# The border between feed-forward and attention: where the layer-norm statistics are made, and who clears and fills the key buffers

## The reference

```
x = x + depool(...)                    # stage 1
x = x + g * ffn(layernorm(x))          # stage 2: per-batch merged weights
x = x + g * attention(layernorm(x), context keys and values)   # stage 3
x = x + g * columns(layernorm(x))      # stage 4

layernorm(x) = (x - mean) / sqrt(var + 1e-5)          # over the 256 columns
attention: qkv = x @ w_qkv.T, 16 heads of 16; k, v = [context, own] (375 + 112 rows)
           softmax(q k^T / 4) v, then @ w_proj.T + b_proj
```

## Time and profile before

| what | value |
|---|---|
| median of three executions | 1504.93 us (1501.84 to 1507.17) |
| profiled execution | 1506.88 us |
| its span | 1505.1 us |
| mean granted TensorE clock | 0.954 |
| busy TensorE, VectorE, ScalarE, GpSimd | 1360.8, 1015.7, 620.0, 546.7 us |
| stage 3 starts | 571.39 us |

### The profile page before, as it was taken

The page is one execution under the profiler, slowest core; times in us unless marked ns, Lnnn a source line. Parts: engine busy times, 40 slices in busy tenths (PEclk is TensorE's granted clock), DMA queues, the critical chain, the costliest instruction groups (busy, mean ns, idle before and its releaser), DMA issues. The chain is left out here.

```text
span 1505.1 us, 33126 instructions
## 1 busy us (share of the span) xinstructions
PE 1360.8 (90%) x12672; PEld 963.5 (64%) x12672; DVE 1015.7 (67%) x1961; ACT 620.0 (41%) x1371; POOL 546.7 (36%) x829
## 2 busy tenths in 40 slices
PE   3687999999999984899999999999999687999997
PEld 3464677777777762567776777667776463555555
DVE  6777665677556764778888888778888543444544
ACT  4433212211221112656666666656666442222221
POOL 0576888888840004323222232222231570000000
PEclk9998999999999996899999999999999688999999
DMA  8205445454531008667667777666672000000000
GB/s 243 66 1 171 132 134 165 124 165 133 162 110 41 32 1 117 123 83 95 84 85 92 97 96 91 84 83 84 84 93 24 0 1 0 13 12 12 20 17 25
DMA packets 92774, 120.25 MB, mean 80 GB/s; under 512 B 7414, under 2 KB 78899, under 8 KB 90348
## 3 DMA queue, kind: packets, MB, share of 16 engines
q1 hardware_dynamic: 83436, 87.82, 34.5%
q0 software_dynamic: 9216, 30.73, 7.0%
HBM read 96.42 MB, written 22.10 MB: 79 GB/s over the span
## 5 line engine op out<-in xcount | busy, mean ns | idle before, releaser
L1123 DVE TENSOR_REDUCE s_neg_max<-banks 112x1 bf16<-112x487 f32 x512 | 323.7, 662 | 92.5 <-PE banks L1234 89.3
L1059 ACT ACTIVATE s_prob<-banks 128x448 f32<-128x448 f32 x512 | 265.9, 547 | 180.2 <-PE banks L1256 180.0
L640 DVE TENSOR_TENSOR s_m<-banks,s_base 128x512 f32<-128x512 f32 x256 | 164.6, 685 | 129.3 <-PE banks L794 129.1
L1234 PE MATMUL banks<-s_k_t,s_q_t 96*112 96x487 bf16 x512 | 198.5, 388 | 1.5 <-DVE s_neg_max L1123 1.5
L1256 PEld LDWEIGHTS banks<-s_q_t,s_k_t 112*128 112x128 bf16 x2048 | 143.4, 99 | 82.1 <-issue 33.9
L1256 PE MATMUL banks<-s_q_t,s_k_t 112*128 112x112 bf16 x2048 | 187.2, 214 | 3.7 <-issue 3.0
L794 PE MATMUL banks<-s_gate_sel,s_tw 64*128 64x256 f32 x1024 | 147.4, 408 | 0.9 <-DVE s_m L640 0.8
L1270 PE MATMUL banks<-s_prob,s_v 128*32 128x112 f32 (+1 forms) x4096 | 129.2, 265 | 7.7 <-issue 7.7
L834 PE MATMUL banks<-s_m,s_act_t 128*112 128x256 f32 x512 | 129.8, 389 | 5.9 <-DVE x_res L659 5.8
L817 PEld LDWEIGHTS banks<-s_x_t,s_m 128*128 128x128 f32 x1024 | 119.1, 192 | 21.2 <-issue 20.9
L817 PE MATMUL banks<-s_x_t,s_m 128*128 128x112 f32 x1024 | 130.5, 281 | 0.0
(11 more groups left out here) (257 smaller groups left out, 2182.7 us busy)
## 6 DMA issues: line engine op xcount, KB each, us to landing
k_parts<-s_k_split POOLq DMA_DIRECT2D x64, 281.2 KB, 3.4
s_k_t<-k_parts SPq DMA_DIRECT2D x32, 562.5 KB, 7.7
s_tw<-in_tw SPq DMA_DIRECT2D x16, 1024.0 KB, 5.1
s_k_raw<-in_ctx_k POOLq DMA_DIRECT2D x64, 187.5 KB, 3.6
s_k_t<-k_parts SPq DMA_DIRECT2D x32, 375.0 KB, 9.9
s_v_raw<-in_ctx SPq DMA_DIRECT2D x32, 256.0 KB
s_src<-in_ctx SPq DMA_DIRECT2D x8, 896.0 KB, 14.4
s_k_t<-k_parts SPq DMA_DIRECT2D x32, 187.5 KB, 11.2
```

What stands on the lines that cost most here:

```text
L640: nc.vector.tensor_tensor(dst[:, :, :, rows_], got, base[:, :, rows_].unsqueeze(2).broadcast_to([P, 2, B, HR]), ALU.add).then_inc(S["merge ...
L1059: nc.scalar.activation(prob[t % 2][:, c, :], w.bank(SCORE + n % SRING, P, TILE), ACT.Exp, scale=DH ** -0.5).then_inc(S["exp_done"], 1)
L1123: nc.vector.tensor_reduce(neg_max[half][:, ROWS + h, 0:1], w.bank(MAX + n % MRING, T, NKEY), AX.X, ALU.max, negate=True).then_inc(S["max_d ...
L1234: nc.tensor.matmul(w.bank(MAX + n % MRING, T, NKEY), q_t[k][0:ROWS, h, :], k_t[k][0:ROWS, h, FIRST:FIRST + NKEY], start=True, stop=True).t ...
```

## The change

1. Stage 2 keeps the statistics of the first eight batches alone: after every second pair, one batch (`early_statistics`).
2. The other 24 are made in stage 3's first turns by VectorE (`late_statistics`): batches 8 to 15 behind `norm(0)`, 16 to 23 behind `split(0)`, 24 to 31 behind `evacuate_queries(0, 0)`.
3. Variance, root and inverse are made in two parts: batches 0 to 7 at the start; for the others the variance stands behind the last statistics, the root on ScalarE behind `evacuate_keys(0, 1)`, the inverse on VectorE behind `evacuate_queries(1, 1)`.
4. ScalarE does one Sqrt of one element behind stage 2's last Gelu.
5. GpSimd clears only the three key edges first, then waits for the first norm and clears the rest. VectorE's `ident16`, `b_proj` and `neg_max` stand behind the first norm.
6. The key rows of buffers 1 and 2 are filled by GpSimd behind `query_parts` of batches 0 and 1. Buffer 0 stays on ScalarE.

```diff
@@ stage 2, VectorE and ScalarE
                     for p in range(PAIRS):
                         added(c, p)
-                        if p:
-                            pair_statistics(p - 1)
-                    pair_statistics(PAIRS - 1)
+                        if p % 2:
+                            early_statistics(p // 2)
+
+                def early_statistics(b):
+                    dve.wait_ge(S["x_done"], nth(PAIRS * (FC - 1) + b // 2))
+                    chain.link(nc.vector.bn_stats(stats[:, b, :], w.x_res[:, b, :]))
+                    nc.vector.bn_aggr(w.mean_var[:, b, :], stats[:, b, :])
...
+                nc.scalar.activation(w.table[:], w.ident[:, 0:1], ACT.Sqrt)
@@ stage 3, GpSimd
                     nc.gpsimd.memset(k_t[k][0:ROWS_MAX, :, 0:FIRST], 0.0).then_inc(S["pads_cleared"], 1)
+                wait(pool, "xn_done", 1)
                 nc.gpsimd.memset(qk[:, 0:H, 6:SLOTS, :], 0.0)
...
+                    if b < 2:
+                        place_heads(b + 1)
+
+                def place_heads(k):
+                    wait(pool, "q_parts_done", k)
+                    nc.gpsimd.tensor_copy(k_t[k][ROWS:ROWS_MAX, :, FIRST:FIRST + S2],
+                                          w.ident[ROWS:ROWS_MAX, ROWS:ROWS_MAX].unsqueeze(2).broadcast_to([H, H, S2]))\
+                        .then_inc(rows_ready[k], 1)
+                    pool.wait_ge(rows_ready[k], 2)
@@ stage 3, ScalarE
+                def roots(first, end, part):
+                    wait(act, "var_done", part)
+                    nc.scalar.activation(root[:, first:end], var[:, first:end], ACT.Sqrt).then_inc(S["root_done"], 1)
+
+                roots(0, EARLY, 1)
...
-                    if b < 2:
-                        place_heads(2 * b)
+                    if b == 0:
+                        place_heads()
...
+                    if (b, n) == (0, 1):
+                        roots(EARLY, B, 2)
@@ stage 3, VectorE
+                def late_statistics(first, end):
+                    for b in range(first, end):
+                        last = nc.vector.bn_stats(late_stats[:, b - EARLY, :], w.x_res[:, b, :])
+                    chain.link(last)
+                    for b in range(first, end):
+                        last = nc.vector.bn_aggr(w.mean_var[:, b, :], late_stats[:, b - EARLY, :])
+                    chain.link(last)
+
+                variances(0, EARLY)
+                inverses(0, EARLY, 1)
...
                     normalised(nc, w, xn[b % 2][:], b).then_inc(S["xn_done"], 1)
-
-                def place_heads():
-
-                    wait(dve, "pads_cleared", 2)
-                    nc.vector.tensor_copy(k_t[1][ROWS:ROWS_MAX, :, FIRST:FIRST + S2],
-                                          w.ident[ROWS:ROWS_MAX, ROWS:ROWS_MAX].unsqueeze(2).broadcast_to([H, H, S2]))\
-                        .then_inc(rows_ready[1], 1)
+                    if b == 0:
+                        prepare()
+                        late_statistics(EARLY, 2 * EARLY)
...
                     if b == 0:
-                        place_heads()
+                        late_statistics(2 * EARLY, 3 * EARLY)
...
+                    if (b, n) == (0, 0):
+                        late_statistics(3 * EARLY, B)
+                        variances(EARLY, B)
+                    if (b, n) == (1, 1):
+                        inverses(EARLY, B, 2)
```

More of the change, by code:

```diff
@@ L56 @@
 CREDIT = 4
+EARLY = 8
 def nth(n):
@@ L134, in __init__ @@
         self.gates = sb("gates", [P, 4])
+        self.table = sb("table", [P, 1])
         self.banks = ctx.enter_context(nc.psum_tensor("banks", [P, 8, 512], F32))
@@ L894, in stage3 @@
         stats = sb("s3_stats", [T, 6])
+        late_stats = sb("s3_late_stats", [T, B - EARLY, 6])
         tmp, root, var = sb("s3_tmp", [T, B]), sb("s3_root", [T, B]), sb("s3_var", [T, B])
@@ L1001, in _, with place_heads @@
             def _(act):
[L1002 to L1008, removed]
+                def roots(first, end, part):
+                    wait(act, "var_done", part)
+                    nc.scalar.activation(root[:, first:end], var[:, first:end], ACT.Sqrt).then_inc(S["root_done"], 1)
+                roots(0, EARLY, 1)
+                def place_heads():
+                    wait(act, "pads_cleared", 1)
+                    nc.scalar.activation(k_t[0][ROWS:ROWS_MAX, :, FIRST:FIRST + S2],
                                          w.ident[ROWS:ROWS_MAX, ROWS:ROWS_MAX].unsqueeze(2).broadcast_to([H, H, S2]),
-                                         ACT.Copy).then_inc(rows_ready[k], 1)
+                                         ACT.Copy).then_inc(rows_ready[0], 1)
                 def evacuate_x(b):
@@ L1089, in _, with variances, inverses, prepare @@
                 chain = Chain(dve, S["chain"])
[L1090 to L1097, removed]
+                def variances(first, end):
+                    nc.vector.tensor_scalar(var[:, first:end], w.mean_var[:, first:end, 1], EPS, None, ALU.add)\
+                        .then_inc(S["var_done"], 1)
+                def inverses(first, end, part):
+                    at_ = slice(first, end)
+                    wait(dve, "root_done", part)
+                    wait(dve, "var_done", part)
+                    chain.link(inverse_root(nc, chain, w.rstd[:, at_, 0], root[:, at_], var[:, at_], tmp[:, at_]))
+                def late_statistics(first, end):
[7 more added lines that the diff above has]
+                inverses(0, EARLY, 1)
+                def prepare():
+                    nc.vector.tensor_copy(ident16[:], w.ident[0:T, 0:T])
+                    dve.wait_ge(w.attention_in, N_WEIGHTS)
+                    nc.vector.tensor_scalar(b_proj[:], b_proj[:], w.gates[0:T, 1:2], None, ALU.mult).then_inc(S["bias_ready"], 1)
+                    for k in range(2):
+                        last = nc.vector.memset(neg_max[k][:], 0.0)
+                    chain.link(last)
                 def norm(b):
```

## The result

The changed kernel took 1496.62 us in the median of 20 executions (1488.19 to 1510.34), the kernel before 1507.51 in 20 (1499.11 to 1520.92). The ratio is 0.992, 95% interval 0.9902 to 0.9937: some 12 us faster, where 6.9 were forecast. The kernel before thus lay 2.6 us above the median that was known ahead. The profiled execution (1503.94, span 1502.2) is one of the slowest of the 20, so I read in it where time goes at the border, not the total.

A forecast was written before the change was run, and what follows sets the result against it. TensorE, busy 90% of the span, was taken as the bound, so only its starved time at the feed-forward/attention border could be won: 8.8 + 2.3 - 1.3 - 2.9 = 6.9 us, from median 1504.93 to 1498.0; range 1492.3 to 1502.5.

The forecast's parts named there:

- Tail: End of the feed-forward: with most statistics gone, TensorE's pairs take 1.03 us instead of 1.575; gain 8.8 us.
- Head: Start of the attention up to the first normalised tile: no table load, norm undisturbed by GpSimd; gain 2.3 us.
- X: Moment the first normalised tile of the attention is ready: S + 5.13 before, forecast S + 2.8.
- S: Start of the attention, 571.39 us in the kernel before; times at its head are counted from it.
- the bound for it: Attention's start: if ScalarE loads its table again, the root starts at S + 1.28 and the gain is 1.7, not 2.3.
- X to Y: Batch 0, from X to TensorE's turning of batch 1 (Y): 18.8 us before, forecast 20.1; loss 1.3.
- The norm of batch 2: VectorE's norm stalls behind GpSimd's second key-row copy (5.2 us), ending at 611.2, not 606.65; loss 2.9 us.
- The rival without the stall: Batch 2's norm does not wait for GpSimd's copy: gain 11.2 us, 1493.7 us; chance 0.17.
- the one with long copies: GpSimd's key-row copies far exceed 5.2 us; from 9.9 us each the change loses, at worst 1510.4; chance 0.06.
- The second stall: Batch 1's norm also waits for GpSimd's first copy, first query evacuation 1.8 us late: 1499.8 us; chance 0.15.
- The sum: All parts together, with the stall at batch 2's norm: 6.9 us gained, 1498.0 us from the median; chance 0.45.
- the best tail: Most favourable bound for the feed-forward's end: 0.98 us a pair, gain 9.5 us.

The follow-up runs named there:

- change without tile: The change without the unused 128 x 1 tile before the attention's buffers and without the Sqrt writing to it; ratio 0.9969 to the kernel before.
- second traces: The kernel before and the changed kernel, each run once more unaltered for another trace; the changed kernel measured 0.9903 against the kernel before.
- four pieces: The change with each of GpSimd's two 16 x 6000 key-row copies made as four of 16 x 1500; ratio 0.9889 to the kernel before.
- the tail both ways: The kernel before with only the feed-forward tail changed (statistics of batches 8 to 31 left out), without and with the tile: 0.995 and 0.9915.

## Why the prediction was right, point by point

1. **Tail.** Forecast 1.03 us a pair and a gain of 8.8; 1.01 and 9.1. Right.
2. **Head.** X forecast at S + 2.8, a gain of 2.3; S + 2.3 and 2.8. Right, the table load went and the norm ran free of GpSimd. The load was worth 0.7 us (change without tile); the bound for it had 0.6.
3. **X to Y.** A loss of 1.3 was forecast, 2.0 came. The eight batches and the variances were right (3.4 us against 3.65); the term that was mis-sized is the first query evacuation, at X + 16.05 and not 15.05. TensorE ended batch 0's queries, keys and values 6.44 us behind X, where it was 5.45. Here is TensorE in the kernel before, then in the change:

```profile
577.72 3.38 PE L1197 MATMUL banks<-s_wqk,s_x_t 128*112 128x512 f32 x4 [0.45 <-ACT s_x_t L1015]
580.94 1.03 PE L1205 MATMUL banks<-s_wv,s_x_t 128*112 128x256 f32 x4
```

```profile
564.15 3.75 PE L1235 MATMUL banks<-s_wqk,s_x_t 128*112 128x512 f32 x4 [0.45 <-ACT s_x_t L1029]
567.70 1.69 PE L1243 MATMUL banks<-s_wv,s_x_t 128*112 128x256 f32 x4
```

   In the trace before, the granted clock was back at 2.4 GHz for the end of it (0.50 from 570.4 to 580.6, then 1.00 until 584), and in the change it was at 0.50 until 569. So ScalarE's copy started 1 us later and ended at X + 12.1. That the clock stepped up just then is chance: in the second traces the values took 1.86 us in the kernel before and 1.19 in the change, the first query evacuation came at X + 15.54, and the loss from X to Y was 1.15 (20.34 - 19.19).
4. **The norm of batch 2.** It was forecast to end behind a copy of 5.2 us begun 0.4 us before it. The copy took 5.18 and the norm 4.90. The loss from the turning of batch 1 to the border's end was 23.45 - 20.63 = 2.8 (3.6 in the second traces); 2.9 was forecast. The rule of the Trainium skill (SBUF — State Buffer, "Who interferes with whom"), that the ports are held for a whole instruction, holds here for one of 5 us too, and four pieces show that the end of a single copy freed them, though others followed. The rival without the stall, and the one with long copies, did not happen.
5. **The second stall** of the rivals did not happen either: the norm of batch 1 took 0.63 us at 572.73 in the trace after, let in between two instructions of GpSimd.
6. **The sum.** 6.9 forecast; at the border 7.1. That it is so close is in part luck: the tail gave 0.3 and the head 0.5 more than forecast, X to Y 0.7 less. But the kernel became some 12 us faster (9.5 to 14.8). What the sum lacks is a term: I priced the Sqrt that uses the new tile, and not the tile, as if an allocation cost nothing (it stands in the kernel, but neither in the list nor in the diff of the change). It moves the key buffers and all others behind it; without it the change is worth 0.9969, which is 4.7 us (interval from a loss of 0.5 to a gain of 9.8) and agrees with the border of that trace, 7.4 to 7.7 us shorter than before. So the total would have lain in the range without the tile too (1504.93 - 4.7 = 1500.2), and the 12 us were not foreseen. The range's lower end doesn't follow from its terms: 11.2 us without the stall and 0.7 for the best tail give 1493.0, not 1492.3.

**What stays open.** The tile shortens the median landing by 0.2 to 0.5 us, but no wait for that landing shows in a steady turn. Where in the attention the 5 to 6 us arise was not found. TensorE stands still at issue in some turns while the key loads are under way; at the same instruction of the same turn it was, in the kernel before and in the second trace of the change,

```profile
1016.33 0.77 PE L1270 MATMUL banks<-s_prob,s_v 128*32 128x112 f32 x20 [2.04 <-issue]
```

```profile
1003.84 0.77 PE L1308 MATMUL banks<-s_prob,s_v 128*32 128x112 f32 x20 [1.54 <-issue]
```

and around the first the granted clock averages 0.88 over 14 us, around the second 1.00. Shorter loads would shorten such stalls, and fewer would cost clock; that is an argument. Summed behind the border (stalls at issue over 0.5 us), they took 12.6 and 13.3 us in the kernel before and 12.4 with the tile, 18.2 with the tail both ways, 18.6 in the change without the tile and 14.5 and 14.7 with it: one of three pairs bears it out. Nor was it tried which displacement of the buffers matters, or whether a larger one gives more.

## What to carry to other kernels

A new instruction on GpSimd has to be laid beside VectorE's list: its price is what is left of it when a VectorE instruction that has to wait for it comes up (here the norm: 4.90 us and not 0.41), if the chain runs through that one. Cutting the copy into four bounded that price at one piece. Work that is moved "behind" a short step should go behind the last one that somebody waits for: eight batches of statistics cost 2.7 to 3.2 us of border in front of the second query evacuation and nothing that shows behind it. And when a measured gain is larger than the trace accounts for, compare things that should not have changed, such as the landing of untouched loads; a new tile may have moved the buffers, and a control with the tile alone shows the landing at once, though it takes many executions to show the time.

## What the runs showed of the hardware that was not expected

With 128 x 1 of float32 more in front of the buffers, the key loads landed sooner: the last of a batch after 10.7 to 10.9 us in ten traces, 11.1 to 11.2 in four without it; the first of a batch, 562.5 KB, took 7.7 to 7.9 either way. That it is the place of the destination in SBUF is the likely reading; other buffers moved too. VectorE's batch statistics ran beside GpSimd's copies at their usual pace (eight in 2.70 us), where the norm and the variances waited for them. VectorE instructions with two SBUF inputs waited for GpSimd as well: in four pieces, two of the small products of the inverse root took 0.59 and 0.66 us while GpSimd copied values and added the bias, and 0.18 each in the change, where GpSimd was idle.
